# Output stores of one kernel for an audio-tower block: a transfer of 127 rows split into one of 112 rows and one of 15

## The reference, cut to what matters

```python
proj = einsum(other, W1) + einsum(readout, W2) + b      # other = X[:, 1:], 255 tokens
h = gelu(proj)                                          # [32, 255, 256]
h = h + attention(layernorm(h))                         # softmax(q k / 8 + bias) v, then o_w
h = h + down(silu(gate(layernorm(h))) * up(layernorm(h)))
return h                                                # [32, 255, 256], float32
```

## Time and profile before

| | |
|---|---|
| median of 3 runs | 1923.34 us (1923.08 to 1924.71) |
| the profiled execution, its own time | 1921.64 us |
| its span, first to last instruction | 1919.8 us |
| PE busy | 1849.5 us, 96% of the span |
| DVE, ACT, POOL busy | 81%, 74%, 52% |
| mean granted clock of PE | 0.99 of full speed |
| DMA issues `out<-h` | 32 of 128 KB and 32 of 127 KB |

### The profile page before, as it was taken

How to read it: one execution, slowest core, us unless ns; L and a number is a source line. 1 busy time by engine, 2 the same in 40 slices (tenths; PEclk the granted TensorE clock), 3 DMA queues, 4 the chain that set the end, 5 groups by cost and what they waited for, 6 DMA issues and landing times.

```text
span 1919.8 us, 42778 instructions
## 1 busy us (share of the span) xinstructions
PE 1849.5 (96%) x15402; PEld 1723.4 (90%) x15402; DVE 1564.0 (81%) x4704; ACT 1422.7 (74%) x3810; POOL 1006.6 (52%) x1359
## 2 busy tenths in 40 slices
PE   4699999999999999999999999999999999999995
PEld 1499999999999999999999999999999999999994
DVE  3488888888888888888888888888888888888884
ACT  5477777777877777777777777777777777777772
POOL 0255555555555555555555555555555555555553
PEclk9799999999999999999999999999999999999997
DMA  6000000000000000000000000000000000000000
GB/s 217 31 10 5 12 15 15 16 15 7 10 16 15 15 15 13 7 12 15 15 16 15 6 11 16 15 15 15 7 10 15 15 15 15 15 5 11 7 7 12
DMA packets 24886, 34.35 MB, mean 18 GB/s; under 512 B 2449, under 2 KB 17810, under 8 KB 24674
## 3 DMA queue, kind: packets, MB, share of 16 engines
q1 hardware_dynamic: 23906, 28.39, 4.9%
q0 software_dynamic: 768, 3.21, 0.4%
HBM read 23.17 MB, written 8.42 MB: 16 GB/s over the span
## 4 chain that ended last, share of the span: by engine, by line
PE 93%; ACT 2%; DVE 1%; DMA 1%; issue 0%; POOL 0%; SPq 0%; POOLq 0%; DVEq 0%
PE ps L487 52%; PE ps L553 13%; PE ps L532 12%; PE ps L542 11%; PE ps L496 3%; PE ps L504 2%; ACT prob L719 1%; DMA out<-h 0%; DVE prob L841 0%; ACT pT L725 0%; DMA r_rows<-readout_rows 0%; DVE pT L850 0%; ACT L719 0%; DVE normed L811 0%; DVE qk L824 0%
## 5 line engine op out<-in xcount | busy, mean ns | idle before, releaser
L719 ACT ACTIVATE prob<-prob,neg_top 128x255 f32<-128x255 f32 x1024 | 508.2, 500 | 67.2 <-DVE neg_top L841 66.8
L445 POOL TENSOR_TENSOR prob<-prob,inv 128x510 f32<-128x510 f32 x512 | 520.4, 1038 | 65.9 <-DVE inv L855 61.8
L450 POOL CAST oT<-heads 128x256 fp32r<-128x256 f32 x256 | 105.8, 413 | 738.1 <-DVE heads L863 738.1
L487 PE MATMUL ps<-xnT,wqk 128*128 128x256 f32 x3072 | 410.5, 283 | 4.1 <-DVE qk L824 2.3
L850 DVE TENSOR_TENSOR pT<-ps,pT 128x512 fp32r<-128x512 f32 x512 | 352.3, 688 | 60.0 <-ACT pT L725 52.9
L487 PEld LDWEIGHTS ps<-xnT,wqk 128*128 128x128 f32 x3072 | 385.3, 189 | 12.4 <-DVE qk L824 3.0
L841 DVE CUSTOM_DVE_ANT_0 prob<-ps,bias 128x255 f32<-128x255 f32 x1024 | 369.8, 417 | 2.1 <-PE ps L532 2.1
L725 ACT ACTIVATE pT<-ps 128x512 fp32r<-128x512 f32 x512 | 302.9, 592 | 26.6 <-PE ps L542 25.0
L553 PE MATMUL ps<-pT,v 128*128 128x256 f32 x2048 | 294.6, 286 | 1.9 <-DVE pT L850 1.9
L553 PEld LDWEIGHTS ps<-pT,v 128*128 128x128 f32 x2048 | 264.8, 189 | 13.1 <-DVE pT L850 1.4
L542 PE MATMUL ps<-ident,prob 128*128 128x128 f32 x2048 | 265.4, 272 | 0.1
(11 more groups left out here) (93 smaller groups left out, 2491.1 us busy)
## 6 DMA issues: line engine op xcount, KB each, us to landing
xt<-x_cols SPq DMA_DIRECT2D x32, 256.0 KB, 2.7
r_rows<-readout_rows SPq DMA_DIRECT2D x32, 128.0 KB, 3.1
out<-h SPq DMA_DIRECT2D x32, 128.0 KB
out<-h SPq DMA_DIRECT2D x32, 127.0 KB
flipped<-bias_rows POOLq DMA_DIRECT2D x1, 3072.0 KB, 16.5
staged<-w_qk SPq DMA_DIRECT2D x8, 256.0 KB, 5.7
staged<-w_v SPq DMA_DIRECT2D x4, 256.0 KB, 7.7
staged<-w_o SPq DMA_DIRECT2D x4, 256.0 KB, 3.1
```

The costliest lines, as they stand in the source:

```text
L445: pool.tensor_tensor(pr, pr, by, ALU.mult).then_inc(prob_done, 1)
L487: mm = pe.matmul(dst, lhs(a, k), rhs(b, k), start=(start and n == 0), stop=(stop and n == last), skip_group_check=skip)
L719: ex = act.activation(pr, pr, ACT.Exp, bias=neg_top[:, g % 2, hh, t:t + 1], scale=-1.0, accum_out=total[:, g % 2, hh, t:t + 1])
```

## The change

The second transfer of each store, rows 128 to 254, is issued as two: rows 128 to 239 (112 rows) and rows 240 to 254 (15 rows). The count that `residual` and SP's last wait look for is moved to three transfers of 16 a batch; the two transfers that fill `h1` ahead of the loop stay. Nothing that is computed is changed, and no wait is added or taken away.

```diff
@@ -56,6 +56,7 @@
 REL = 2 * T - 1
 WINDOW = T + P
+EVEN = S // 16 * 16
@@ -407,7 +408,8 @@
                 def store(batch):
                     sp.wait_ge(out_done, count(1, batch))
                     sp.dma_start(out[batch, 0:P, :], h1[:, 0, :]).then_inc(out_free, 16)
-                    sp.dma_start(out[batch, P:S, :], h1[0:S - P, 1, :]).then_inc(out_free, 16)
+                    sp.dma_start(out[batch, P:EVEN, :], h1[0:EVEN - P, 1, :]).then_inc(out_free, 16)
+                    sp.dma_start(out[batch, EVEN:S, :], h1[EVEN - P:S - P, 1, :]).then_inc(out_free, 16)
@@ -421,7 +423,7 @@
                 store(B - 1)
-                sp.wait_ge(out_free, 32 * (B + 1))
+                sp.wait_ge(out_free, 32 + 48 * B)
@@ -865,7 +867,7 @@
                 def residual(batch):
                     dve.wait_ge(op_mm, count(1, batch))
-                    dve.wait_ge(out_free, count(32, batch, 31))
+                    dve.wait_ge(out_free, 32 + 48 * batch)
```

## The result

The change makes the kernel faster: a median of 1912.86 us (1911.73 to 1915.06, 6 runs) against 1923.24 (1922.26 to 1924.71, 6 runs), ratio 0.9947 with a 95% interval of 0.9934 to 0.9960, that is 7.7 to 12.7 us. Timed again later it was 1914.12 against 1923.47, ratio 0.9949 (0.9935 to 0.9963). The profiled execution took 1914.30 us, 7.34 less than the profiled one of before.

What follows compares the result with a forecast made beforehand. PE was taken to bound the kernel, busy 1849.5 of 1919.8 us, with only the last two stores on the path. Gains 5.5 + 3.6 = 9.1 us, clock and middle zero, took 1923.34 to 1914.2 us, range 1911.7 to 1916.5.

Steps and rivals of the forecast that it cites:

- The last store: End of the span: batch 31's store lands earlier, gain 5.5 us, range 3.85 to 5.8 (third transfer hidden behind the second).
- the small write: Last store's landing judged by `readout_rows<-r_sb`: 1.7 us from issue to landing, so 1914.13 and a gain of 5.25.
- my count of packets: Last store's landing from packets per engine at 0.047 us a row: 1913.8, which is 5.6 us earlier than 1919.38.
- The store of batch 30: Before the last residual: L869 starts after PE's last `project`, at 1889.80 instead of 1893.43, 3.63 us earlier (3.6 taken).
- The clock: PE's clock in the last block: still falls to half and the block starts at half as now, zero effect.
- a clock that stays up: Last block: if PE's clock didn't fall, transposes save about 0.4 and product groups some 1.9, 2.3 us in all.
- The middle: The 30 middle stores: 15 us of DVE's waits go away, but PE is always busy, so zero gain.
- The sum: Whole kernel: 5.5 + 3.6 = 9.1 us, from 1923.34 to 1914.2 us; both terms as counted given 0.74.
- no effect: Rival, stores: 112 rows still go over one engine or transfers serialize, 1923.3 to 1924.2 us; chance 0.09.
- the middle gives too: Rival, middle batches: PE paced by DVE, up to 15 us of waits come back, 1899 us; chance 0.05.
- rows cut fine: Rival, the 15 rows: moved in pieces of one value, 12 us per engine, slower at 1935.8 us; chance 0.03.
- the clock helps: Rival, last block: shorter PE idling keeps the clock up or returns it earlier, up to 2.3 us, 1911.9; chance 0.09.

Runs made afterwards that it cites:

- 113 + 14 rows: Every store issued as 128 + 113 + 14 rows, against the kernel before the change: median 1922.22 us (1922.81 beside it), ratio 0.9996 (0.9987 to 1.0005).
- the five kernels with this gain: Kernels without work for PE whose last two stores are spread over many engines, against the kernel before: all five gained 8.5 to 10.2 us.

## Why the prediction was right, point by point

**The last store.** Forecast 5.5 us (3.85 to 5.8); 5.21 in the profile, 4.6 timed alone. The step was right: the 47 small packets of a store fit 112 rows over sixteen engines and 15 over fifteen. It was 0.3 us too good in two places. The issues start 0.40 and 0.47 us apart where I had put 0.37 twice, so the third starts 0.87 us after the first (1909.60 to 1910.47) instead of 0.74. And it lands 1.6 us after its issue, not 1.4, which is nearer to the 1.7 us of the small write than to my count of packets; all bytes took 1.3 us from the first, where I had about 0.9. The span ends 2.0 us after the last issue starts, not 1.8. The landing at 1919.38 was assumed from the other store, and is confirmed only now. The 5.8 us that I gave as the upper end follows from no working there: the count gives 5.6 to 5.7.

The Trainium skill's price (DMA: Bandwidth & Descriptors, "Anatomy of one DMA — SWDGE (gpsimd) path": about 2.0 us fixed) is a fit for transfers issued from GpSimd, which the prediction left out. The estimate from it was too high for these stores from SP: 1.6 to 1.8. The skill's row against two transfers to disjoint halves of the partitions (same page, "Rules for kernel authors") gives as its reason that both halves go over all 16 engines. Here that was not so, the 127 rows went over one (1.06 by the earlier trace rows), and the split paid.

**The store of batch 30.** Forecast 3.63; 3.62 in the profile, 3.3 timed alone. PE's last projection is the next releaser, as said.

**The clock.** Forecast zero, with 0.4 to 0.8 us lost if it came back later in the block. It came back 4.9 us after `gate_up` started (1897.36 to 1902.3) instead of 4.1 (1899.83 to 1903.9), and the block took 0.38 us more. In other profiles of kernels with a half-clock start the 48 products took 7.56 to 8.37 us, so this term differs from run to run, to both sides of the 7.73 of before. The 2.3 us that I put on a clock that stays up came out: with PE kept busy the block takes 15.91 us against 18.23 before. One reason of mine was weak: that the clock would fall at half a microsecond into the gap as before. It fell after 1.1. That it falls at all, with only 3.9 us of idling, held in every profile in which PE was left idle there.

**The middle.** Forecast zero; a batch takes 56.87 us as before, and the kernel with these 30 stores alone is unchanged. The kernel with only two stores split is as fast as the change, and the 1704.23 us of the profiles leave nothing for the middle.

**The sum.** 9.1 us forecast, 1914.2; measured 1912.86 and 1914.12, both inside the range of 1911.7 to 1916.5, with gains of 10.2 and 9.8 by the ratios. From the two profiles the effect is 5.21 + 3.62 - 0.38 = 8.45 us, which lies in the intervals of both timings. What the medians show above that, some 1.4 to 1.8 us, is left open: it is within their uncertainty, two of the five kernels with this gain show 8.5 and 8.8 us, and the start of the program and the clock in the last block move single profiled executions by 3.8 and by 0.8 us. That 9.1 lies between the account of the profiles and the medians is in part luck. In the range, 1912.8 to 1916.0 doesn't follow from the two gains with 0.7 us on each side, which gives 1913.2 to 1916.6; the measured 1912.86 is inside the stated range either way. The rivals fell: no effect (that is what 113 + 14 rows look like), the middle gives too, rows cut fine (255 packets of a row each). That the clock helps is no part of the change, but it can be had with it.

## What to carry to other kernels

In every store tried here, a transfer whose row count has no large divisor went over few DMA engines: count the small packets of one transfer, or see whether a DMA queue moves at about 22 GB/s for microseconds. Splitting off a remainder so that the rest divides by 16 costs an issue of 0.4 us on the queue and is worth it only where somebody waits for the landing: here in 2 of 32 stores, at the end, while 15 us of waits on an engine with slack were worth nothing. Before believing such a gain, look for what is late next (here PE's last projection, whose end then released the residual), and where an engine idles for microseconds ahead of the last block, its clock is the next thing to look at.

## What was not expected of the hardware

- A DMA issue on SP takes longer for some shapes: 0.29 us for 127 rows, 0.34 for 128, 0.43 for 112 and 0.45 for 15 rows of 1 KB.
- Issuing the last store's transfers from two queues at once brought the last bytes forward by 0.2 us and the landing by nothing; each transfer took 0.4 to 0.5 us longer to land.
- Whether PE's clock is back at full when the second group of query and key products starts, some 70 us into the program, differs between executions, though no store has been issued by then (1.67 or 2.93 us for twelve products). It makes about 2 us of difference in the total, a fifth of the effect studied here.
